# Spare products of the identity on TensorE, in the last attention batch and at the start of the experts

## The chip, the cores and the metric

The kernel runs on one NeuronCore of a Trainium2 chip. The metric is the time of one execution on the device in microseconds. The engines are TensorE (PE in the profile; PEld is its loading of weights), VectorE (DVE), ScalarE (ACT), GpSimd (POOL) and SyncE (SP), each with its own queue of instructions, tied to the others by semaphores. TensorE's clock is granted by the chip at one of two levels, 1.2 and 2.4 GHz; the profile gives the granted clock as a share of the full one.

## The reference

One decoder block over x of 4 x 512 tokens by 512 features, in float32:

```
x = x + attention(layernorm(x))     # 16 heads of 32, a band of 128 keys and 4 sinks, biases, output projection
x = x + experts(layernorm(x))       # silu(h @ c.T) * (h @ c.T) @ c, with c = ctx[expert of the token's id], 4 experts
x = x + bit_ffn(layernorm(x))       # 8-bit activations, ternary weights, hidden size 2048, rms norm
```

In the expert part the matrix c of 512 x 512 is the gate, the up and the down weight at once.

## The kernel before

The kernel has three phases that follow each other. The change touches the end of the first and the start of the second.

**Attention** (`attention_phase`). The four batches are worked one after another. Within a batch, four groups of four heads (g) by four tiles of 128 queries (qt) make 16 units. The round of a batch is g = 1 to 4; g = 4 is the first group of the next batch, so the last batch (b = 3) has rounds g = 1 to 3 only. PE's order is written out in `unit` (line 1026). Unit (g, qt) first makes the scores of the next unit into `s_ps` (`scores`, line 945: three products per head, float32 split in a high and a low part, then the band's mask), which waits until ACT has exponentiated the scores before them. Then it transposes the first two of its own four slots of probabilities (`transpose_slot`, line 967), does one product of a projection on the side (`side`, line 931: parts X, Q, K, V and O, into the bank `side_ps`), transposes slots three and four, and after every second unit multiplies the transposed probabilities by V (`attend_pair`, line 1009; the last products are those of the sinks). Slots one and three go through the first half of `pT_ps` and are copied out by ACT, slots two and four through the second half and are copied out by DVE; so slot three waits for ACT's copy of slot one, slot four for DVE's copy of slot two. In the last unit of a group the fourth slot is the widened reciprocal of the sums.

DVE's order per unit is in its own `unit` (line 749): the two maxima of the next unit's scores (line 725), the norm of the group before in units (g, 0), the copy of slot two, the side work, the copy of slot four; in units (2,1), (2,2), (2,3) and (3,0) of the last batch also an addition of the output bias to `xres` (line 797). ACT's is in line 570: the copy of slot one, four exponentials with their sums, the copy of slot three. POOL widens the reciprocals, splits the attention output in high and low (lines 412 to 424) and, in the last batch, splits the experts' matrices (lines 453 to 465), which are four large operations on 128 x 2048 elements on POOL and two on DVE.

In the last batch the side work ends with K3, the projection of the last keys, in unit (1,3); DVE ends its split with line 651 and counts `side_left` up. Units (2,0) to (3,1) have no side work. In unit (3,2) PE begins the output projection (`o_begun`, line 1020) into `side_ps` and free banks of `s_ps`; its last part, after the last split, is line 1085. Then the phase's block of programs ends: all engines meet, after SP and ACT have stored the last rows.

**Experts** (`expert_phase`). POOL gathers the tokens' rows by expert in 19 tiles of 128 (line 1317). For each tile DVE makes the statistics and normalizes (lines 1410 to 1424), PE transposes (`transpose_x`, line 1504), ACT and DVE make the high and low part (lines 1370 and 1428), PE multiplies by c (`expert_product`, line 1516: 12 matmuls of 128 x 512 into `z_ps`), ACT applies silu (line 1387), DVE multiplies (line 1464), PE transposes the result (line 1554), and 12 further matmuls make y (`y_of`, line 1526). PE's order is that of `tensor_program` (line 1503): the sums of the weights' absolute values (line 1534), then ten products of the identity with itself into `y_ps` whose result nobody reads (line 1536, the number is `KEPT_BUSY["experts"]` of line 37), the first transpose, and the loop over the tiles.

Of the kernel before, what the change touches and what calls it, by code (L numbers as in the profile page):

```python
# [10 lines left out]
P = 128  # L11
BATCH, SEQ, D = 4, 512, 512
# [3 lines left out]
HG = HEADS // GH  # L16
# [17 lines left out]
OWN_TILES = ROUTED_TILES - 2 * TT - FRONT_HOMES  # L34
X_LATE = 11
GATHERS_AHEAD = 6
KEPT_BUSY = {"experts": 10}
ROUTE_COUNTED, ROUTE_STEPS, ROUTE_DENSE = 10, 34, 42
LISTED = 2
BO_UNITS = [(2, 1), (2, 2), (2, 3), (3, 0)]  # L40
# [19 lines left out]
def attention_phase(nc, io, x1, x2, slot_tokens, dense_tokens, sh):  # L60
# [7 lines left out]
    with ExitStack() as ctx:  # L68
# [3 lines left out]
        def ps(name, shape, dt=F32):  # L72
            return ctx.enter_context(nc.psum_tensor(name, shape, dt))

        def sem(name):
            return ctx.enter_context(nc.semaphore(name))

        ident, rows, expert_of = sh["ident"], sh["rows"], sh["expert_of"]
# [73 lines left out]
        pT_ps = ps("pT_ps", [P, 2, GH * P])  # L152
        pv_ps = ps("pv_ps", [P, SEQ])
        side_ps = ps("side_ps", [P, SEQ])
# [9 lines left out]
        side_done, side_hi, side_left = sem("side_done"), sem("side_hi"), sem("side_left")  # L164
# [41 lines left out]
        def place_of(qt):  # L206
            return slice(QUERY_PLACE[qt] * P, QUERY_PLACE[qt] * P + P)
# [21 lines left out]
        def taken(b, name):  # L229
            return name not in LATE if b == 0 else name in LAST if b == BATCH - 1 else True  # L230
# [16 lines left out]
        def projected(b, g, qt):  # L247
            name = PROJECTED[g].split()[qt]
            return None if name == "-" or (g and not taken(b, name)) else name
# [32 lines left out]
        with nc.Block() as block:  # L282
# [608 lines left out]
            def _(pe):  # L891
                def product(out, steps, first, final):

                    terms = [(lt[i], r[j]) for lt, r in steps for i, j in ((0, 0), (0, 1), (1, 0))]
                    for n, (lt, r) in enumerate(terms):
                        last = nc.tensor.matmul(out, lt, r, start=(first and n == 0), stop=(final and n == len(terms) - 1))  # L896
                    return last
# [6 lines left out]
                def project(name, out, blocks_):  # L904

                    i = int(name[1])
                    rows, cols = slice(i * P, i * P + P), slice(i * P, i * P + P)
                    if name[0] == "O":
                        rows = place_of(i)
                    steps = []  # L910
                    for k in blocks_:
                        if name[0] in "QK":
                            n = name[0].lower()
                            steps.append(((w_hi[n][:, k, cols], w_lo[n][:, k, cols]), (xT_hi[:, k, :], xT_lo[:, k, :])))
                        elif name[0] == "V":
                            steps.append(((xT_hi[:, k, rows], xT_lo[:, k, rows]), (w_hi["v"][:, k, :], w_lo["v"][:, k, :])))
                        else:
                            steps.append(((aT_hi[:, k, rows], aT_lo[:, k, rows]), (w_hi["o"][:, k, :], w_lo["o"][:, k, :])))
                    return product(out, steps, blocks_[0] == 0, blocks_[-1] == DK - 1)
# [47 lines left out]
                def transpose_slot(b, g, qt, k):  # L967
                    slot = slots_of(qt)[k]
                    if copies_before(b, g, qt, k):
                        pe.wait_ge(slot_copied[k % 2], copies_before(b, g, qt, k))  # L970
                    if k == 0:
                        pe.wait_ge(exp_done, units_before(b, g, qt) * GH + GH)
                    if slot == "rinv":
                        pe.wait_ge(rinv_widened, b * HG + g + 1)
                        for t in range(TT):
                            last = nc.tensor.transpose(pT_ps[:, 1, place_of(t)], norm[:, t * P:t * P + P], ident[:])
                    elif slot == "sink":
                        pe.wait_ge(sinks_gathered, 2 * (b * HG + g) + qt - 1)
                        last = nc.tensor.transpose(pT_ps[0:GH * SINKS, 0, 0:P], sinks[:].rearrange("p h n -> p (h n)"), ident[:])
                    else:  # L980
                        a, z = columns(qt, slot)
                        for h in range(GH):
                            last = nc.tensor.transpose(pT_ps[:, k % 2, h * P:h * P + P], weights[qt][:, h, a:z], ident[:])  # L983
                    last.then_inc(slot_transposed, 1)
# [35 lines left out]
                def o_begun(t):  # L1020
# [2 lines left out]
                        pe.wait_ge(attn_split, BATCH * HG - 1)  # L1023
                    project(f"O{t}", o_banks[t], whole[:-1])

                def unit(b, g, qt, last):
                    nxt = (g, qt + 1) if qt + 1 < TT else (g + 1, 0)
                    if not (last and nxt == (HG, 0)):
                        scores(b, *nxt)
                    transpose_slot(b, g, qt, 0)  # L1030
                    transpose_slot(b, g, qt, 1)
                    name = projected(b, g, qt)
                    if name:
                        side(b, nth_in(b, g, name), name)
                    if last and g == HG - 1 and qt >= 2:
                        o_begun(qt - 2)
                    transpose_slot(b, g, qt, 2)
                    transpose_slot(b, g, qt, 3)
                    if last and (g, qt) == (HG - 1, TT - 1):
                        o_begun(2)  # L1040
                    if qt % 2:
                        attend_pair(b, g, qt - 1)
                    name = turned(b, g, qt)
                    if name:
                        side(b, nth(b, name), name)
# [37 lines left out]
                pe.wait_ge(attn_split, BATCH * HG)  # L1083
                for t in range(TT):
                    project(f"O{t}", o_banks[t], whole[-1:]).then_inc(o_projected, 1)


def landed(s):
# [136 lines left out]
def expert_phase(nc, ctx, scratch, io, x1, x2, sh, front):  # L1225
# [19 lines left out]
    ident, rows, expert_of = sh["ident"], sh["rows"], sh["expert_of"]  # L1245
# [18 lines left out]
    gate = big("gate", [P, D])  # L1264
# [5 lines left out]
    y_ps = front.y_ps  # L1270
# [20 lines left out]
    def inside(s):  # L1291
        return 0 <= s < ROUTED_TILES
# [210 lines left out]
    def tensor_program(pe):  # L1503
        def transpose_x(s):
            pe.wait_ge(xn_ready, s + 1)
            if inside(s - 1):
                pe.wait_ge(xT_lo_ready, s)
            for k in range(DK):
                last = nc.tensor.transpose(xT_ps[:, k, :], xn[:, s % 2, k * P:k * P + P], ident[:])  # L1509
            last.then_inc(xn_transposed, 1)  # L1510

        def weights_of(s):

            return nc.tensor.value_load(expert_of[0:1, one(s)], min_val=0, max_val=(EXPERTS - 1) * DK)

        def expert_product(out, hi, lo, first):

            n = 0
            for k in range(DK):
                at = bass.ds(first + k, 1)  # L1520
                for lt, r in ((hi, c_hi), (hi, c_lo), (lo, c_hi)):
                    last = nc.tensor.matmul(out, lt[:, k, :], r[:, at, :], start=(n == 0), stop=(n == 3 * DK - 1))  # L1522
                    n += 1
            return last

        def y_of(s):
            first = weights_of(s)

            pe.wait_ge(aT_lo_ready, s + 1)
            expert_product(y_ps[:], aT_hi, aT_lo, first).then_inc(y_ready, 1)  # L1530

        pe.wait_ge(consts, 3)
        pe.wait_ge(row_summed, 1)
        nc.tensor.matmul(sum_ps[:], e_ones[:], abs_row[:], start=True, stop=True).then_inc(all_summed, 1)
        for n in range(KEPT_BUSY["experts"]):
            nc.tensor.matmul(y_ps[:, 0:P], ident[:], ident[:], start=True, stop=True)
        transpose_x(0)

        for s in range(ROUTED_TILES):
            first = weights_of(s)  # L1540
            pe.wait_ge(xT_lo_ready, s + 1)
            if inside(s - 1):
                pe.wait_ge(a_ready, s)
            expert_product(z_ps[:], xT_hi[:, s % 2], xT_lo[:, s % 2], first).then_inc(z_ready, 1)
            if s == 0:
                transpose_x(1)
            if inside(s - 1):
                y_of(s - 1)
            if s == ROUTED_TILES - 1:
                pe.wait_ge(front.consts, 4)  # L1550
                front.transpose_x(pe, 0)
            pe.wait_ge(a_ready, s + 1)
            for k in range(DK):
                last = nc.tensor.transpose(aT_ps[:, k, :], act_sb[:, k * P:k * P + P], ident[:])  # L1554
            last.then_inc(a_transposed, 1)
            if inside(s + 2):
                transpose_x(s + 2)

        pe.wait_ge(w_ready, CHUNKS)
        front.first_gate(pe)  # L1560
        y_of(ROUTED_TILES - 1)
        front.transpose_x(pe, 1)
# [427 lines left out]
```

## Time and profile before

| what | value |
|---|---|
| median of 3 runs | 792.04 us (791.56 to 792.66) |
| span of the profiled execution, first to last instruction | 789.9 us; its own time outside the profiler isn't shown |
| TensorE busy | 735.5 us, 93% of the span, 5130 matmul records |
| VectorE, ScalarE, GpSimd busy | 597.9, 471.4, 333.0 us |
| mean granted clock of TensorE | 0.976 of 2.4 GHz |

The span is divided by the page into 40 slices of 19.7 us. The last attention batch's units (2,0) to (3,3) lie between 398 and 449 us, the last output projection ends at 454.6, the experts' phase begins at about 457.6 and lasts until about 600. A float32 product of the identity stands as two matmul records, a transpose as one.

### The profile page before, as it was taken

To read this page: it belongs to the slowest core of one execution; us is meant where nothing else is said; L and a number is where in the kernel's file an instruction comes from. 1 tells how busy PE (TensorE), PEld (TensorE's weight loads), DVE (VectorE), ACT (ScalarE), POOL (GpSimd) and SP (SyncE) were. 2 spreads that over 40 slices of the span, in tenths; PEclk is the share of its full clock that TensorE was granted. 3 is DMA by queue.
4 is the path that set the end of the run, shared out by engine and by line. 5 is a ranking of instruction groups with operands and counts; after the bars stand their busy time and mean duration, and the time that the engine had idled before them with its cause. 6 is when DMAs were issued, how large, how long until landed. Compare 5 with 4: busy or idle time off the path is not lost. (4 is left out here: it accounts for less than half of the span.)

```text
span 789.9 us, 14108 instructions
## 1 busy us (share of the span) xinstructions
PE 735.5 (93%) x5130; PEld 509.0 (64%) x5130; DVE 597.9 (76%) x1102; ACT 471.4 (60%) x1024; POOL 333.0 (42%) x330
## 2 busy tenths in 40 slices
PE   5988999999999999999987959999998999999984
PEld 4766777777777777777755747888874444444431
DVE  6886766886668866766677547887888999999982
ACT  5555766666667666766555214444455777667761
POOL 2011204213142134454373343445546667777662
PEclk9999999999999999999997979999999999999998
DMA  9200021304030331215330075455430233333231
GB/s 319 108 1 28 27 66 70 108 28 161 28 108 28 108 134 54 81 55 189 107 108 1 2 252 198 176 194 202 149 120 31 53 82 94 88 99 97 77 80 54
DMA packets 55218, 78.33 MB, mean 99 GB/s; under 512 B 36335, under 2 KB 38383, under 8 KB 53424
## 3 DMA queue, kind: packets, MB, share of 16 engines
q1 hardware_dynamic: 46336, 51.99, 20.2%
q0 software_dynamic: 8528, 24.93, 9.1%
q8 instruction: 43, 0.70, 0.4%
q10 hardware_dynamic: 288, 0.52, 0.2%
q14 instruction: 23, 0.19, 0.1%
HBM read 56.92 MB, written 17.59 MB: 94 GB/s over the span
## 5 line engine op out<-in xcount | busy, mean ns | idle before, releaser
L556 ACT ACTIVATE probs<-s_ps,neg_max 128x512 f32<-128x512 f32 (+2 forms) x256 | 152.3, 610 | 20.3 <-DVE neg_max L725 18.6
L725 DVE TENSOR_REDUCE neg_max<-s_ps 128x2 f32<-128x1024 f32 (+2 forms) x128 | 124.5, 1014 | 33.1 <-PE s_ps L963 32.6
L983 PE MATMUL pT_ps<-ident,probs 128*128 128x128 f32 x832 | 116.6, 282 | 9.3 <-DVE probs L746 8.3
L568 ACT ACTIVATE probs<-pT_ps 128x512 f32<-128x512 f32 x96 | 57.4, 598 | 98.6 <-PE pT_ps L983 97.8
L983 PEld LDWEIGHTS pT_ps<-ident,probs 128*128 128x128 f32 x832 | 95.0, 145 | 24.7 <-DVE probs L746 11.0
L746 DVE COPY probs<-pT_ps 128x512 f32<-128x512 f32 x112 | 76.8, 685 | 36.8 <-PE pT_ps L983 36.8
L1681 POOL TENSOR_TENSOR xg_own<-h,ln_w_sb 128x512 f32<-128x512 f32 x64 | 83.9, 1322 | 33.9 <-DVE h L1767 33.8
L896 PE MATMUL side_ps<-w_hi 128*128 128x512 f32 x172 | 71.1, 414 | 0.0
L420 POOL TENSOR_TENSOR aT_hi<-norm,one_col 128x512 fp32r<-128x512 f32 x15 | 15.6, 1040 | 125.4 <-DVE norm L737 87.1
L896 PE MATMUL side_ps<-w_hi,w_lo 128*128 128x512 f32 x172 | 67.5, 392 | 0.0
L896 PE MATMUL side_ps<-w_lo,w_hi 128*128 128x512 f32 x172 | 67.1, 390 | 0.0
L1875 PE MATMUL y_ps<-w_tern,hqT 128*128 128x512 bf16 x240 | 61.0, 380 | 2.6 <-DVE v_next L1809 2.6
L1005 PE MATMUL pv_ps<-probs,v_sb 128*32 128x256 f32 (+1 forms) x896 | 53.0, 373 | 0.4 <-ACT probs L568 0.4
L556 ACT ACTIVATION_READ_ACCUMULATOR probs<-s_ps,neg_max 128x1 f32 x256 | 52.8, 206 | 0.0
L1724 ACT ACTIVATE hq<-hq_big,minus_offset 128x1024 bf16<-128x1024 f16 x30 | 33.1, 1143 | 30.9 <-DVE hq_big L1804 30.9
L412 POOL TENSOR_TENSOR norm<-rinv,one_col 128x512 f32<-128x512 f32 x16 | 16.7, 1042 | 82.4 <-DVE rinv L732 82.4
L1875 PEld LDWEIGHTS y_ps<-w_tern,hqT 128*128 128x128 bf16 x240 | 22.9, 98 | 28.1 <-issue 3.0
L1643 PE MATMUL e_xT_ps<-w_tern,xqT_home 128*128 128x512 bf16 x128 | 33.0, 380 | 6.8 <-DVE h L1767 6.2
L1773 DVE TENSOR_REDUCE hw_max<-xg_own 128x1 f32<-128x1024 f32 x32 | 38.7, 1209 | 0.2
L1005 PEld LDWEIGHTS pv_ps<-probs,v_sb 128*32 128x32 f32 x896 | 25.5, 111 | 18.0 <-issue 6.0
L896 PEld LDWEIGHTS side_ps<-w_hi,w_lo 128*128 128x128 f32 x172 | 32.3, 188 | 7.3
L1387 ACT ACTIVATE gate<-e_z_ps 128x512 f32<-128x512 f32 x19 | 11.4, 598 | 42.0 <-PE e_z_ps L1522 42.0
(285 smaller groups left out, 1800.1 us busy)
## 6 DMA issues: line engine op xcount, KB each, us to landing
w_piece<-w_ffn SPq DMA_DIRECT2D x24, 512.0 KB, 3.5
w_stage<-w_ffn SPq DMA_DIRECT2D x12, 1024.0 KB, 4.8
xres<-x POOLq DMA_DIRECT2D x4, 1024.0 KB, 5.7
xn<-x SPq DMA_DIRECT2D x3, 1024.0 KB, 8.5
x<-xres POOLq DMA_DIRECT2D x3, 1024.0 KB, 4.8
xn<-c SPq DMA_DIRECT2D x2, 1024.0 KB, 6.1
v_next<-c SPq DMA_DIRECT2D x2, 1024.0 KB, 7.9
xn<-x SPq DMA_DIRECT2D x4, 256.0 KB, 3.5
```

The lines of the kernel that those rows point to most:

```text
L556: nc.scalar.activation(weights[qt][:, h, at:at + width(qt)], s_ps[:, h, 0:width(qt)], ACT.Exp, bias=neg_max[:, qt % 2, h:h + 1], accum_out ...
L568: nc.scalar.activation(out, turned_p, ACT.Identity).then_inc(slot_copied[0], 1)
L725: nc.vector.tensor_reduce(neg_max[:, qt % 2, 2 * s:2 * s + 2], s_ps[:, 2 * s:2 * s + 2, 0:width(qt)], AX.X, ALU.max, negate=True).then_inc ...
L746: nc.vector.tensor_copy(weights[qt][:, :, a:z], pT_ps[:, 1, :].rearrange("p (h n) -> p h n", h=GH))\
L896: last = nc.tensor.matmul(out, lt, r, start=(first and n == 0), stop=(final and n == len(terms) - 1))
L983: last = nc.tensor.transpose(pT_ps[:, k % 2, h * P:h * P + P], weights[qt][:, h, a:z], ident[:])
L1005: last = nc.tensor.matmul(pv_ps[HD * h:HD * h + HD, to], v_sb[:, slot, f:f + HD], p, start=first, stop=final, tile_position=(0, HD * h))
L1643: last = nc.tensor.matmul(out[:], xqT[:, t % 2, k, :], weights[:, k, cols], start=(k == 0), stop=(k == DK - 1))
L1681: nc.gpsimd.tensor_tensor(hw[:, t % 2, c, :], h[:, t % 2, c, :], ln_w[:, c * CHK:c * CHK + CHK], ALU.mult)\
L1724: nc.scalar.activation(hq[:, cols], hq_code[:, cols], ACT.Identity, bias=minus_offset[:]).then_inc(hq_packed, 1)
L1773: nc.vector.tensor_reduce(hw_max[:, i, n:n + 1], flat(hw, i)[:, n * HALF:n * HALF + HALF], AX.X, ALU.max, apply_absolute_value=True).then_ ...
L1875: last = nc.tensor.matmul(sums_of(t), hqT[:, t % 2, k, :], down_w[:, k, :], start=(k == 0), stop=(k == FK - 1))
```

## The change

The dictionary of numbers gets four new entries and another value for the experts. In the last attention batch, in units (2,0) to (3,1), PE makes four products of the identity with itself ahead of the next unit's scores and four behind the transposes of the first two slots, into `side_ps`; ahead of the first four it waits until K3 has been taken out of that bank. Ten more are made into `pT_ps` behind the last output projection. In front of the first transpose of the experts stand 24 instead of ten, behind it nine, and behind the second transpose seven, all into `y_ps`. No result of them is read.

```
-KEPT_BUSY = {"experts": 10}
+KEPT_BUSY = {"unit": 4, "end": 10, "experts": 24, "first split": 9, "first gate": 7}
...
+                def keep_busy(bank, where):
+                    for n in range(KEPT_BUSY[where]):
+                        nc.tensor.matmul(bank, ident[:], ident[:], start=True, stop=True)
+
                 def unit(b, g, qt, last):
                     nxt = (g, qt + 1) if qt + 1 < TT else (g + 1, 0)
+                    spare = last and (2 <= g < HG) and (g, qt) < (HG - 1, 2)
+                    if spare:
+                        pe.wait_ge(side_left, nth(BATCH - 1, "K3"))
+                        keep_busy(side_ps[:, 0:P], "unit")
                     if not (last and nxt == (HG, 0)):
                         scores(b, *nxt)
                     transpose_slot(b, g, qt, 0)
                     transpose_slot(b, g, qt, 1)
+                    if spare:
+                        keep_busy(side_ps[:, 0:P], "unit")
                     name = projected(b, g, qt)
...
                 for t in range(TT):
                     project(f"O{t}", o_banks[t], whole[-1:]).then_inc(o_projected, 1)
+                keep_busy(pT_ps[:, 0, 0:P], "end")
...
         nc.tensor.matmul(sum_ps[:], e_ones[:], abs_row[:], start=True, stop=True).then_inc(all_summed, 1)
-        for n in range(KEPT_BUSY["experts"]):
-            nc.tensor.matmul(y_ps[:, 0:P], ident[:], ident[:], start=True, stop=True)
+
+        def keep_busy(where):
+            for n in range(KEPT_BUSY[where]):
+                nc.tensor.matmul(y_ps[:, 0:P], ident[:], ident[:], start=True, stop=True)
+
+        keep_busy("experts")
         transpose_x(0)
+        keep_busy("first split")
 
         for s in range(ROUTED_TILES):
...
             if s == 0:
                 transpose_x(1)
+                keep_busy("first gate")
             if inside(s - 1):
                 y_of(s - 1)
```

## Rows read from the trace of the kernel before

**Rows 1.** The page: the span.

```profile
span 789.9 us, 14108 instructions
```

**Rows 2.** Stretches: us, busy us (records) of PE, PEld, DVE, ACT, POOL, clock, DMA share, GB/s.

```profile
403.80:407.20 3.40, 3.40 (x26) 2.63 (x25) 1.67 (x3) 0.64 (x3) 3.32 (x3) 0.53 0.02 5
...
417.50:424.30 6.80, 5.95 (x45) 3.46 (x41) 4.67 (x8) 3.39 (x10) 1.04 (x1) 0.52 0.01 2
...
431.10:434.50 3.40, 3.12 (x16) 2.49 (x15) 3.09 (x4) 2.30 (x8) 3.40 (x2) 0.53 0.00 0
...
458.40:465.20 6.80, 5.27 (x25) 5.27 (x26) 2.38 (x7) 0.69 (x1) 5.12 (x8) 0.51 0.48 133
...
472.10:475.50 3.40, 1.98 (x12) 1.29 (x11) 2.73 (x6) 2.18 (x4) 0.42 (x1) 0.97 1.02 419
```

**Rows 3.** Timeline, the spares before: start, length (us), engine, instruction, [idle before].

```profile
459.93 0.58 PE L1534 MATMUL up_ps<-abs_row,e_ones 128*128 128x3 f32 x2 [5.33 <-POOL e_ones L1335]
460.38 4.62 PE L1536 MATMUL y_ps<-ident 128*128 128x128 f32 x20
```

**Rows 4.** Timeline of PE: transposes of (2,2) and (2,3), attend products of (2,3) and (3,3).

```profile
412.53 1.04 PE L983 MATMUL pT_ps<-ident,probs 128*128 128x128 f32 x8
...
416.65 0.51 PE L955 MATMUL s_ps<-k_hi,q_hi 32*128 32x512 f32 x4
...
417.75 1.97 PE L983 MATMUL pT_ps<-ident,probs 128*128 128x128 f32 x8
...
421.99 2.29 PE L1005 MATMUL pv_ps<-probs,v_sb 128*32 128x256 f32 x24
...
447.39 1.29 PE L1005 MATMUL pv_ps<-probs,v_sb 128*32 128x256 f32 x24
```

**Rows 5.** Timeline, PE and DVE: unit (2,0) and the start of (2,1).

```profile
398.28 0.50 PE L955 MATMUL s_ps<-k_hi,q_hi 32*128 32x512 f32 x3
...
398.91 0.21 DVE L651 SCALAR_TENSOR_TENSOR k_lo<-side_ps,bk_sb,k_hi 128x4 fp32r<-128x4 f32 x1
...
399.90 1.23 DVE L725 TENSOR_REDUCE neg_max<-s_ps 128x2 f32<-128x1024 f32 x1 [0.78 <-PE s_ps L963]
...
403.51 1.07 PE L983 MATMUL pT_ps<-ident,probs 128*128 128x128 f32 x4 [1.75 <-DVE probs L746]
```

**Rows 6.** Timeline, PE, DVE, POOL: units (2,1), (2,2), (3,0), (3,1).

```profile
409.76 3.61 POOL L458 TENSOR_TENSOR w_hi<-xn,one_col 128x2048 fp32r<-128x2048 f32 x1
...
410.02 3.90 DVE L797 TENSOR_TENSOR xres<-xres,bo_sb 128x512 f32<-128x512 f32 x1
...
411.73 0.40 PE L955 MATMUL s_ps<-k_hi,q_hi 32*128 32x260 f32 x4
...
413.84 1.29 DVE L725 TENSOR_REDUCE neg_max<-s_ps 128x2 f32<-128x520 f32 x2
...
429.47 0.66 PE L983 MATMUL pT_ps<-ident,probs 128*128 128x128 f32 x4 [1.75 <-DVE probs L746]
...
431.11 2.86 PE L983 MATMUL pT_ps<-ident,probs 128*128 128x128 f32 x12
431.77 1.82 DVE L725 TENSOR_REDUCE neg_max<-s_ps 128x2 f32<-128x776 f32 x2
...
436.76 0.39 PE L955 MATMUL s_ps<-k_hi,q_hi 32*128 32x260 f32 x4
```

**Rows 7.** Timeline of PE: the first matmul of the first expert product.

```profile
467.38 0.49 PE L1522 MATMUL e_z_ps<-w_hi,e_xT_hi 128*128 x1 [1.86 <-DVE e_xT_lo L1428]
```

**Rows 8.** The chain in order of time: start us, us, what.

```profile
467.38 4.60 PE e_z_ps L1522 x12
...
473.44 0.65 PE e_aT_ps L1554 x4
...
475.12 4.59 PE e_z_ps L1522 x12
...
483.35 2.76 PE e_z_ps L1522 x12
```

## The prediction

> **What bounds the kernel now.** I read four views, in this order. First the page: a span of 789.9 us [rows 1]; the median of the runs shown, 792.04, is 2.1 us above it, and I put the sum on that median. Then the stretches around the falls [rows 2]: the clock stands at its lower level, 1.2 GHz, in 403.8 to 407.2, 417.5 to 424.3 and 431.1 to 434.5 (last attention batch), and in 458.4 to 465.2 (start of the experts). The first two expert products are slow as well, 4.60 and 4.59 us for 12 matmuls that later take 2.76 [rows 8]. Each fall follows idle time of PE, each return follows steady work. The four stretches are 20.5 us; half clock can have cost no more than half of that and the 3.7 us of the two products, and less where PE waits for others anyhow. Third, the timeline of the last batch: per unit PE makes the scores, VectorE (DVE) takes two maxima, ScalarE (ACT) four exponentials, and PE's next scores need those. Both PE's order and DVE's set the pace. Last, the chain: it runs over DVE to the first expert product [rows 7] and from there almost wholly over PE [rows 8], so what is lost or won there reaches the end whole.
>
> **The price of a spare product.** Ten products stand as 20 records in 4.62 us, the last record's own tail included: 0.43 us each at 1.2 GHz [rows 3]. No row has one at 2.4 GHz. Eight transposes of the same 128x128 shape take 1.97 us at the low clock and 1.04 at the high one [rows 4], so I take half: 0.21 us each, 0.85 for four. The bounds are 0.85 and 1.7 for four; I take the low one, as the spares follow other work of PE.
>
> **Part 1, four in front of the scores, units (2,0) to (3,1).** PE stood idle before none of these scores (no idle time is written beside them [rows 4 to 6]): its waits lie before the later transposes. So these four lie on the path.
> - Unit (2,0). The new wait is for K3's split, which DVE ends at 398.91 + 0.21 = 399.12; in the profile the scores began at 398.28, and DVE idled 0.78 us until it could start the maxima at 399.90 [rows 5]. Now the scores start at about 399.15 + 0.85 = 400.0: +1.75 us. Behind the waiting PE stand only these scores; DVE and ACT wait for them.
> - Unit (2,1). +0.85. What the clock gives back: from the last transposes to the scores two units on took 403.51 to 411.73, 8.22 us, against 429.47 to 436.76, 7.29, in the next round, where less of it was slow: -0.93. Near zero in sum.
> - Unit (2,2). Here DVE's addition to xres took 3.90 us next to POOL's 3.61 us copy of an expert's matrix, which had begun 0.26 earlier, and ended 0.55 after it; the maxima came only at 413.84, while the scores (from 411.73) were done about 1.1 us before [rows 6]. The four fit in that 1.1. POOL's work hangs on DVE's norm of unit (2,0), so it comes later by the same 1.75. Shift stays +1.75.
> - Unit (2,3). +0.85, as the scores start at 416.65 behind the transposes with nothing between [rows 4]. Back at full clock: about 0.15 in the scores, 0.5 in the four transposes of the reciprocals (half of 1.97 less 1.04), 1.0 in the attend products (24 took 2.29 here, 1.29 at full clock [rows 4]). Sum +1.75 + 0.85 - 1.65 = +0.95.
> - Unit (3,0). +0.85, and 0.1 because scores no longer overlap the products of the sinks: +1.9.
> - Unit (3,1). +0.85, of which DVE hides about 0.5: it took the maxima at 431.77 only, while PE had left the scores for the transposes at 431.11 [rows 6]. The slow transposes there (2.86 us for 12) lie beside DVE's maxima. Sum about +2.2.
> After it no spare is put in and the clock was full until the end of the stage: the stage ends **2.2 us later**. If the clock falls all the same, nothing comes back: 1.75 + 0.85 + 0 + 0.85 + 0.95 + 0.35 = +4.75, and up to about +8 with the fours behind the first at 1.7 each. If DVE's addition slips in ahead of POOL's copy (the 0.26 us above), about 0.5 less.
>
> **Part 2, four behind the first transposes of these units.** PE waits there for DVE anyhow, 1.75 us before the fourth slot's transposes in units (2,0) and (3,0) [rows 5, 6]; in (2,1) and (3,1) up to 0.2 us could show. Taken as zero; at 1.2 GHz 1.7 us would fill the whole cover.
>
> **Part 3, ten behind the output projection.** PE is idle for 5.33 us, from 454.6 until it is wanted at 459.93 [rows 3]. Ten at 0.21 take 2.1 us, or 4.3 at most. Zero, as the gather and the stores hide it. They leave 3.2 us of idle time, not 5.3; a slow product followed on 1.86 us of idle time as well [rows 7], so I don't count on their holding the clock.
>
> **Part 4, 24 instead of ten, nine behind the first transpose.** Times here are from the spares' start at 460.38. In the profile ten took about 4.3, and the first expert product began at +7.0, behind DVE's low part of the transposed row [rows 7]. Of the stretches at the lower level two lasted 3.4 us and two 6.8 [rows 2]. With 3.4 us of it the 24 take 8 x 0.43 + 16 x 0.21 = 6.8; with 4.86 (460.38 to 465.24, as here) 7.5; all low 10.3; all high 5.1. I take 6.8. Then four transposes (0.5), and nine spares (1.9, where the path over ACT's and DVE's copies took 1.86 [rows 7]): the product begins at +9.25, which is 2.25 us later. Given back: its 12 matmuls take 2.76 instead of 4.60 us [rows 8], -1.84.
>
> **Part 5, seven behind the second transpose.** 0.45 + 1.5 us, where the path over ACT and DVE to the transposed product takes 1.45 [rows 8]: +0.5. The second expert product then runs at full clock: 2.76 for 4.59, -1.83. Sum of parts 4 and 5: 2.25 - 1.84 + 0.5 - 1.83 = **-0.9 us**. From there on PE is busy and at full clock as before.
>
> **Sum.** +2.2 - 0.9 = +1.3, over 792.04: 793.3 us. About 0.2% (1.6 us) is what a measurement of this kernel can tell from no change; the forecast lies just inside it.
>
> A rule that speaks against the change: the row shows that in 431.1 to 434.5 PE did next to nothing but transposes, and that the clock was back at 434.5 [rows 2, 6]. The Trainium skill, "TensorE: Matmul & The Clock Gate", Part 4: PE-mode transpose, says that transposes don't count as busy time for the clock. By it four spares between long rows of transposes could be too little and the clock would fall in the units all the same; the trace disagrees in the place named. The time that this would give is the first rival's.
>
> **The rivals.**
> 1. *Slower: the clock falls in the units all the same*, since a spare group of 0.85 us leaves PE idle for the rest of each wait. Place: units (2,0) to (3,1). Price: +4.75 for the stage (above), -0.9 behind it: 795.9. Against it: with 0.85 of the 1.75 us waits filled, no unbroken idle time of the length seen before a slow stretch is left. For it: in 472.1 to 475.5 PE was busy for 1.98 of 3.4 us, in pieces [rows 2], and the product from 475.12 on was slow [rows 8]. It decides from two falls left in the units on.
> 2. *Slower, milder: the 24 run mostly at 1.2 GHz.* They end at +9 to +10.3 instead of +6.8: +2.2 to +3.5 over the forecast, 795.5 to 796.8. For it: the ten of the profile ran so from first to last [rows 3]. Against it: the clock was back 4.9 us after they began.
> 3. *Faster: the front four cost less than written*, because DVE is what PE waits for in more units than (2,2) and (3,1), for instance where DVE gets ahead of POOL, and because other executions lost more to the low clock than the profiled one. Stage +0.2, experts -2.6 (the 24 all at full clock, 5.1 us, so 1.7 less): 789.6. For it: up to 13 us stand to be won. Against it: the wait in unit (2,0), which nothing hides.
> 4. *The change doesn't do what it says:* the falls at the experts' start stay as they are, spares gain nothing there: +2.2 and +2.75: 797. Against it: steady spares brought the clock back at 465.2.
>
> **How the numbers follow.** Forecast and its neighbourhood (791 to 794.5) 0.55; rival 1 0.12; rival 2 0.10; rival 3 0.18; rival 4 0.05. Range: from 789.6 (rival 3's figure) to 796.2 (rivals 1 and 2); it leaves out rival 4 and the tails. Faster by over 0.2% (below 790.5): most of rival 3 and a little of the forecast's lower side, 0.18. Slower (above 793.6): rivals 1, 2, 4 and a third of the forecast, 0.40. Same: 0.42.
>
> **What the changed profile would show.** Right: no stretch at 1.2 GHz in units (2,0) to (3,1); 32 records of spares per pair of units at about 0.11 us apart; the maxima of unit (2,0) about 1.8 us later against the batch's start; PE's last output projection 2.2 us later; an idle stretch of some 3 us after the ten; the first expert product some 9.3 us after its spares' start; both first expert products in 2.76 us. Wrong: idle time of PE in front of the spares of other units than (2,0) (then they are hidden), the maxima at their old distance, falls between 398 and 435, or a first expert product more than 10 us behind the start of its spares.

## The result, and the profile after

The changed kernel took 795.16 us (median of 6 executions, 794.14 to 796.57), the kernel before on the same chips 791.57 (6, 786.52 to 792.66). The ratio is 1.0074, with a 95% interval of 1.0048 to 1.0099: 0.7% slower. The six times of the kernel before are far apart (three at 791.6 to 792.7, one at 786.5), so the two medians differ by 3.6 us only, while the ratio stands for 5.9. Repeated, it was 794.64 against 788.49 (6 and 26 executions), ratio 1.0070 (1.0042 to 1.0098), which is 5.5 us by the ratio and 6.2 by the medians. I had forecast +1.3 us; it is about +6.

Of the page after, the span and TensorE's granted clock in 40 slices:

```profile
span 794.8 us, 14443 instructions
...
PEclk9998999999999999999999999999999999999997
```

The spans differ by 4.9 us. The stretches of the changed kernel answer to [rows 2]; columns are us, busy us (records) of PE, PEld, DVE, ACT, POOL, clock, DMA share, GB/s:

```profile
398.00:403.80 5.80, 5.58 (x60) 3.65 (x60) 2.24 (x5) 2.54 (x9) 3.60 (x1) 1.00 0.35 142
403.80:435.00 31.20, 26.69 (x273) 21.25 (x272) 23.18 (x28) 17.29 (x50) 13.18 (x7) 1.00 0.11 36
435.00:459.00 24.00, 23.58 (x191) 17.34 (x190) 14.01 (x22) 7.55 (x23) 10.11 (x4) 1.00 0.02 6
459.00:464.40 5.40, 2.40 (x21) 2.20 (x19) 1.07 (x3) 1.28 (x1) 1.29 (x4) 1.00 0.47 173
464.40:467.80 3.40, 3.30 (x15) 3.31 (x16) 1.03 (x3) 0.00 (x0) 2.00 (x4) 0.50 0.59 159
467.80:484.00 16.20, 16.01 (x114) 14.54 (x113) 8.90 (x21) 3.51 (x7) 7.06 (x12) 1.00 0.90 329
```

The clock is at 2.4 GHz through all units and both first expert products. In this part of the kernel one fall of 3.4 us is left, at the start of the experts' spares. So the change does what it says, and the kernel is slower.

The timeline of the changed kernel (PE, DVE, POOL; start, length, engine, instruction, idle before) answers to [rows 5, 6]:

```profile
401.51 1.16 PE L1028 MATMUL side_ps<-ident 128*128 128x128 f32 x8 [0.22 <-DVE k_lo L651]
...
403.82 2.36 DVE L725 TENSOR_REDUCE neg_max<-s_ps 128x2 f32<-128x1024 f32 x2 [2.36 <-PE s_ps L963]
...
409.96 1.84 DVE L725 TENSOR_REDUCE neg_max<-s_ps 128x2 f32<-128x776 f32 x2 [1.15 <-PE s_ps L963]
413.75 4.10 DVE L797 TENSOR_TENSOR xres<-xres,bo_sb 128x512 f32<-128x512 f32 x1
...
413.69 3.61 POOL L458 TENSOR_TENSOR w_hi<-xn,one_col 128x2048 fp32r<-128x2048 f32 x1
...
417.78 1.29 DVE L725 TENSOR_REDUCE neg_max<-s_ps 128x2 f32<-128x520 f32 x2
```

DVE's idle time ahead of the first maxima grew from 0.78 to 2.36 us: that is the wait for K3 and the four spares. The addition to xres begins 0.06 us behind POOL's copy and waits for it. The chain of the changed kernel at the start of the experts, in order of time, answers to [rows 8]; the last line is not of the chain but of PE's timeline and answers to [rows 7]:

```profile
465.08 6.84 PE y_ps L1549 x48
471.93 0.44 PE e_xT_ps L1520 x4
472.36 2.01 PE y_ps L1549 x18
474.37 2.77 PE e_z_ps L1533 x12
477.14 0.44 PE e_xT_ps L1520 x4
477.57 1.56 PE y_ps L1549 x14
479.13 0.44 PE e_aT_ps L1571 x4
...
474.13 0.48 PE L1533 MATMUL e_z_ps<-w_hi,e_xT_hi 128*128 x1
```

Here the chain runs over the spares themselves; before, it ran over the gather and DVE.

The next table is worked out from the timelines: differences between the starts of DVE's first maxima of consecutive units (the unit's number is that of the scores they read), then from the start of the sum's matmul (the instruction ahead of the experts' spares) to the first expert product z0, from there to the second z1 and to the first y. The first column is from the maxima of the second batch's first unit to those of (2,1); the last is the sum of the columns. The starts of z0, z1 and y0 are those of the timeline. From (3,3) to the sum's matmul it was 22.3 us in all of them, which is left out.

| kernel, profiled execution | to (2,1) | (2,1) to (2,2) | to (2,3) | to (3,0) | to (3,1) | to (3,2) | to (3,3) | to z0 | to z1 | to y0 | sum |
|---|---|---|---|---|---|---|---|---|---|---|---|
| before | 266.19 | 6.32 | 7.62 | 4.08 | 7.94 | 5.91 | 5.88 | 7.44 | 7.74 | 4.43 | 323.55 |
| before, again | 266.18 | 5.25 | 5.93 | 4.15 | 6.53 | 5.91 | 7.59 | 7.39 | 7.52 | 2.86 | 319.31 |
| changed | 267.78 | 6.14 | 7.82 | 4.52 | 7.83 | 6.15 | 5.93 | 9.63 | 6.07 | 2.86 | 324.73 |
| behind the transposes only | 266.23 | 5.26 | 5.94 | 4.16 | 6.52 | 5.91 | 5.88 | 7.44 | 6.11 | 2.86 | 316.31 |

Against the first row the change costs 1.2 us, as forecast (+1.3). The other 3.7 us of the span lie where no spare stands: 2.2 in the first batch, where the changed execution had two falls of the clock (at 58.2 and 71.9) and the first one had one (65.7), and 1.5 at the end, where it had one more (775.0). But the first row is not what the kernel before usually does: its second profiled execution, the second row, is 4.2 us better in the same stretches. In the four jobs of the experiments the kernel before ran 119 times beside the others, with a median of 789.1; only 12 of these reached 791.5, the region of all three times I had.

### The profile page after: what moved, and what is told of

Read it like the earlier page. It is cut to its first block and busy times, and to the rows that moved or that the text cites. A ratio compares the mean times of both kernels' runs of the same rounds, so it can differ in the third digit from the quotient of the medians.

```text
span 794.8 us, 14443 instructions
## 1 busy us (share of the span) xinstructions
PE 746.8 (94%) x5289; PEld 522.5 (66%) x5306; DVE 598.9 (75%) x1102; ACT 471.7 (59%) x1024; POOL 333.1 (42%) x330
## 3 DMA queue, kind: packets, MB, share of 16 engines
q1 hardware_dynamic: 46336, 51.99, 20.5%
## 5 line engine op out<-in xcount | busy, mean ns | idle before, releaser
L983 PE MATMUL pT_ps<-ident,probs 128*128 128x128 f32 x832 | 112.6, 275 | 8.2 <-DVE probs L746 7.7
L983 PEld LDWEIGHTS pT_ps<-ident,probs 128*128 128x128 f32 x832 | 91.8, 141 | 22.4 <-DVE probs L746 10.3
L896 PEld LDWEIGHTS side_ps<-w_hi 128*128 128x128 f32 x172 | 32.4, 188 | 5.8 <-DVE k_lo L651 0.6
```

## The experiments

The experiments ran in four jobs, and the kernel before ran beside the others in each; ratios are against it. Medians of different jobs differ by some tenths of a microsecond for the same kernel: the kernel before had 788.87, 788.49, 789.45 and 788.93.

**The kernel before again, and the change in two halves.**

> The kernel before, unchanged, as a control. Theory A (the clock's falls move from run to run): its times spread over several us again, between about 786 and 793 as so far, and the profile shows its falls of the granted clock in other places than the first one did, with the last batch's VectorE and GpSimd operations shifted against each other. Theory B (the changed kernel pays somewhere that no spare stands): the times stay near 792 and the falls stand where they stood.

Measured: 789.38 us (785.4 to 794.02, 12 executions); ratio 1.0012 (0.9987 to 1.0038), the kernel compared with itself. Its profile has the clock low at 427.9 to 434.7 and nowhere else in the units. Its addition, by the timeline of DVE and POOL:

```profile
409.74 1.44 DVE L797 TENSOR_TENSOR xres<-xres,bo_sb 128x512 f32<-128x512 f32 x1
...
410.58 4.05 POOL L458 TENSOR_TENSOR w_hi<-xn,one_col 128x2048 fp32r<-128x2048 f32 x1
```

It came 0.84 us ahead of the copy, and this time POOL waited. Its 1.44 us, where such an addition takes 0.68 elsewhere, are a wait as well: POOL's operation ahead of the copy ran until 410.63. So theory A holds: the falls move from execution to execution, and with them this order.

Only the spares in the units:

```
-KEPT_BUSY = {"unit": 4, "end": 10, "experts": 24, "first split": 9, "first gate": 7}
+KEPT_BUSY = {"unit": 4, "end": 0, "experts": 10, "first split": 0, "first gate": 0}
```

> Only the four and four spares in units (2,0) to (3,1). Theory A (my sum, each part priced against the falls of one execution): from the end of K3's split to PE's last output projection 2.1 us more than the 55.5 us of the first profile, the experts' start as slow as before; over the median of before by about 3, since the median execution lost less to the clock in the units than the profiled one. Theory B (the cost lies in the experts' part): within 1 us of before.

Measured: 792.84 us (12) against 788.87, ratio 1.0057 (1.0034 to 1.0080). From the end of K3's split to the last output projection it took 57.7 us for 55.5, as theory A said; against the median of before it is 4.0 us slower, where A said about 3. The profile shows the addition at 4.10 us. So most of the loss lies here.

Only the spares around the experts (`spare = False`, the numbers of the changed kernel else):

> Only the ten behind the output projection, the 24, nine and seven; none in the units. Theory A: 1.1 us less than before from the spares' start to the second tile's matmuls if the first two expert products are at 1.2 GHz in before, up to 2.5 us more if they are at full clock there anyhow; median within 1.5 us of before. Theory B: slower by 3 or more, as the first expert product waits for the spares.

Measured: 788.49 (12), ratio 0.9987 (0.9963 to 1.0011). No loss and no gain that can be told. In its profile the clock didn't fall at the experts' start at all; PE's timeline there:

```profile
461.73 5.61 PE L1549 MATMUL y_ps<-ident 128*128 128x128 f32 x48
```

The 24 took 5.6 us, last record's tail included, and z0 came 8.05 us after the sum's matmul. The units of this kernel are those of before, and this execution (792.01, the slowest of its twelve) looks like the first profile there: falls at 405.3, 418.9 and 432.6, and the addition 0.02 us behind the copy and 4.14 us long. In both, the fall near 404 had made the step from (2,1) to (2,2) longer than the 5.25 us of full clock, by 1.07 and 0.84 us. Less the 0.84 us by which the addition is ahead at full clock, this makes it 0.2 and 0.0 us late, where the rows have 0.26 and 0.02. So in the kernel before, the clock's fall itself can turn the order.

**The spares behind the transposes alone.** The four in front of the scores are left out, and so are all the experts' new ones:

```
-                    if spare:
-                        pe.wait_ge(side_left, nth(BATCH - 1, "K3"))
-                        keep_busy(side_ps[:, 0:P], "unit")
                     if not (last and nxt == (HG, 0)):
...
                     if spare:
+                        pe.wait_ge(side_left, nth(BATCH - 1, "K3"))
                         keep_busy(side_ps[:, 0:P], "unit")
```

> Only the four spares behind the first two slots' transposes in units (2,0) to (3,1), with the wait for K3's split moved there (free, as the split is done by then). Theory A: PE waits there anyhow, so they cost nothing; the clock may be held in part of the falls; 0 to -2 us against before. Theory B (every spare delays the chain): +2 to +5 us.

Measured: 785.27 (784.47 to 786.28, 12), ratio 0.9954 (0.9936 to 0.9972): faster than both kernels, and its 12 times spread over 1.8 us where the 35 of before spread over 9.7. The stretch of its units:

```profile
398.00:435.00 37.00, 31.82 (x361) 24.00 (x350) 26.90 (x38) 21.72 (x64) 24.31 (x10) 1.00 0.10 30
```

The clock is at full speed without one product in front of any scores. The last row of the table is what the units take then. Against it the products in front cost 1.6 us up to unit (2,1) and 4.7 from there to (3,3), 6.3 us in the profiles. Step by step the 4.7 are 0.9, 1.9, 0.4, 1.3, 0.2 and 0.1: the second is the step with the late addition, and the fourth is 0.4 more than four products, which no run here explains. By the medians of this job (792.84 and 785.27) the products in front cost 7.6 us, so their price is known to about a microsecond.

**The changed kernel again, and the addition moved out of the way.**

> The changed kernel, unchanged, for a ratio over many executions. Theory C (the fours in front of the scores make VectorE's addition to xres in unit (2,1) come just behind the start of GpSimd's copy and so wait for all of it, 4.1 us instead of 1.4, in every execution; before pays that in some executions only): 0.4 to 0.7% slower than before, with a narrow spread of its own but for falls of the clock in the first batch and at the end; the addition takes about 4.1 us in the profile. Theory A (only the sum of the parts as forecast, +1.3): 0.1 to 0.2% slower.

Measured: 794.64 (793.78 to 795.59, 6), ratio 1.0070 (1.0042 to 1.0098). The addition took 4.10 us again, in the same place.

```
-BO_UNITS = [(2, 1), (2, 2), (2, 3), (3, 0)]
+BO_UNITS = [(2, 2), (2, 3), (3, 0), (3, 2)]
```

> The changed kernel with VectorE's four additions of the bias in units (2,2), (2,3), (3,0) and (3,2) instead of (2,1), (2,2), (2,3) and (3,0), so none stands where GpSimd copies the experts' matrices in unit (2,1). Theory C: from the maxima of unit (2,0) to those of unit (2,2) 11 to 12 us instead of 13.96; 2 to 3 us faster than the changed kernel. Theory A: no change beyond 0.7 us (the addition itself).

Measured: 793.76 (9), ratio 1.0067 (1.0046 to 1.0089). A miss for theory C in its size: from (2,1) to (2,3) it took 13.17 us for 13.96, not 11 to 12; from (2,2) to (2,3) 7.03 for 7.82. Once the addition is gone PE is what the maxima wait for: its four spares of unit (2,2), which had lain in the addition's shadow, come out.

> The same move in the kernel before. Theory C: the executions in which the addition came late disappear, the median falls by 1 to 2 us and the highest of the times by 2 or more. Theory A: same as before, with the same spread of some 9 us, as the clock alone makes it.

Measured: 788.19 (784.98 to 789.5, 12), ratio 0.9984 (0.9966 to 1.0002). The highest time fell as theory C said (789.5, where 8 of the 26 times of the kernel before in the same job lie above it, up to 792.19). The median fell by 0.3, not by the 1 to 2 that C said. This fits a late addition that makes the tail of before, and in part of its executions only; twelve times are few to show it.

One product fewer in front of unit (2,1):

```
-                        keep_busy(side_ps[:, 0:P], "unit")
+                        keep_busy(side_ps[:, 0:P], 3 if (g, qt) == (2, 1) else "unit")
```

> The changed kernel with three products instead of four in front of the scores of unit (2,1), and nothing else. The addition began 0.06 us behind GpSimd's copy in the changed kernel; one product less is 0.25 us. Theory C: the addition now comes about 0.2 us ahead and takes 1.4 us; 1.5 to 3 us faster than the changed kernel for one product less, at least in most executions. Theory A: 0.25 us faster.

Measured: 793.63 (12), ratio 1.0059 (1.0041 to 1.0076). The addition slipped ahead (0.78 us long). (2,1) to (2,3) took 12.95 us for 13.96: one product of 0.22 us brought 1.0, again cut short by the four of unit (2,2).

**The same threshold where nothing else covers it.** To the spares behind the transposes four or three products are added in front of unit (2,1) alone:

```
+                    if last and (g, qt) == (2, 1):
+                        pe.wait_ge(side_left, nth(BATCH - 1, "K3"))
+                        for n in range(4):
+                            nc.tensor.matmul(side_ps[:, 0:P], ident[:], ident[:], start=True, stop=True)
```

> The spares behind the transposes, and four in front of the scores of unit (2,1) alone. VectorE's addition began 0.83 us ahead of the start of GpSimd's copy without them, and four products are 0.86 us. Theory D: the addition falls behind the start of the copy and waits for it, 4.1 us for 1.4; from the maxima of unit (2,1) to those of (2,2) 8 us instead of 5.9, in all 2.7 to 3 us slower than 785.3. Rival (the products cost only their own time): 0.9 slower.

> As the kernel with four in front of unit (2,1), with three. Theory D: the addition stays 0.2 us ahead of the copy and takes 0.7 to 1 us; 0.7 us slower than 785.3 at most, so one product, 0.22 us of PE's time, is worth 2 us or more here. Rival: 0.22 us between three and four.

Measured: 789.54 with four (12; ratio 0.9998, 0.9981 to 1.0015), 787.10 with three (12; 0.9972, 0.9954 to 0.9991). The timelines of DVE and POOL, with four:

```profile
406.24 1.84 DVE L725 TENSOR_REDUCE neg_max<-s_ps 128x2 f32<-128x776 f32 x2 [1.15 <-PE s_ps L963]
410.03 4.09 DVE L797 TENSOR_TENSOR xres<-xres,bo_sb 128x512 f32<-128x512 f32 x1
414.04 1.29 DVE L725 TENSOR_REDUCE neg_max<-s_ps 128x2 f32<-128x520 f32 x2
...
409.97 3.60 POOL L458 TENSOR_TENSOR w_hi<-xn,one_col 128x2048 fp32r<-128x2048 f32 x1
```

and with three:

```profile
406.95 1.84 DVE L725 TENSOR_REDUCE neg_max<-s_ps 128x2 f32<-128x776 f32 x2 [0.93 <-PE s_ps L963]
410.74 0.76 DVE L797 TENSOR_TENSOR xres<-xres,bo_sb 128x512 f32<-128x512 f32 x1
412.88 1.31 DVE L725 TENSOR_REDUCE neg_max<-s_ps 128x2 f32<-128x520 f32 x2 [1.39 <-PE s_ps L963]
...
410.91 4.05 POOL L458 TENSOR_TENSOR w_hi<-xn,one_col 128x2048 fp32r<-128x2048 f32 x1
```

With four the addition begins 0.06 us behind the copy and the maxima follow 7.80 us after the last ones; with three it begins 0.17 ahead and they follow after 5.93. Together with the products themselves, four cost 2.8 us from (2,1) to (2,3) and three 0.7. The fourth, 0.22 us of PE, costs 2.1 us in the profiles and 2.4 by the medians. Theory D holds: this pair of kernels differs by one product and by the order it sets. Both medians are about 1.2 us higher than expected; the kernel before was 0.6 higher in this job too, and the rest isn't accounted for.

**The wait in unit (2,0), and all but the front.**

> The spares behind the transposes, and four in front of the scores of unit (2,0) alone, behind the wait for K3's split. Theory D: the maxima of unit (2,0) come 1.6 us later, nothing else moves, median 786.9. Rival (the wait is hidden behind VectorE's split, which uses the same engine): within 0.9 of 785.3.

Measured: 788.45 (12), ratio 0.9988 (0.9969 to 1.0007). The path up to (2,1) took 267.79 us for 266.23, +1.56, and the columns from there to (3,3) are those of the table's last row: the mechanism and its price as said. The median is 1.5 above the 786.9 expected; in the profile the step from z0 to z1 took 7.71 us for 6.11, as the clock fell there, which is this much, but whether it does so in most executions wasn't seen.

> The changed kernel without any of the 24 products in front of scores (the fours behind the transposes, the ten, 24, nine and seven all stay). Theory D (the loss lies in the products in front of the scores, 6.3 us with the wait for K3's split and with VectorE's late addition; the 24 cost 2 us or more beyond what they give back once the clock is held anyway): median about 787.5, 6 to 7 us faster than the changed kernel and 2 to 2.5 slower than the spares behind the transposes alone (785.3). Rival (the experts' spares pay for themselves): at or below 785.3.

Measured: 788.15 (12), ratio 0.9986 (0.9965 to 1.0007). Near theory D's 787.5 (it is 3.0 us above the fours behind alone, for the 2 to 2.5 of the theory), and 6.5 us below the changed kernel's 794.64 of the other job (6.6 by the two ratios). In its profile the clock didn't fall at the experts' start, and z0 came after 8.05 us.

**Which of the experts' spares cost.** Each group is added by itself to the spares behind the transposes (only the numbers of `KEPT_BUSY` differ).

> The spares behind the transposes alone, again, beside variants on the same chip. Theory D (they hold the clock in the units at no cost): 3 to 4 us faster than before again, spread under 3 us. Rival (the first result was a lucky phase of the clock): within 2 us of before, spread of 4 us or more.

> The same and the ten products behind the output projection. Theory D: hidden, 0; if they shorten the fall of the clock so that the first ten of the experts' spares and the first two expert products run at full clock, up to 1.6 us faster in the executions where those are slow otherwise. Rival: they hold up the end of the stage, slower by 1 or more.

> The spares behind the transposes, and 24 instead of ten at the experts' start, without the ten, nine and seven. Theory D: the first expert product begins 7.6 to 9.5 us after the spares' start, where it is 7.5 with ten, since the 24 outlast the gather and the normalization when they start at 1.2 GHz; 0.5 to 2 us slower than the spares behind the transposes alone. Rival: the held clock gives it back, no slower.

> The spares behind the transposes, ten at the experts' start as before, and nine and seven behind the first two transposes. Theory D: nine and seven lie almost wholly in PE's waits (0.1 and up to 0.5 us show) and keep the first two expert products at full clock: 0 to 1 us faster than the spares behind the transposes alone in executions where those products were slow, else 0.4 slower. Rival: they delay both products, 1 us or more slower.

| kernel | median us | ratio to before | 95% interval |
|---|---|---|---|
| behind the transposes | 785.16 (6) | 0.9955 | 0.9938 to 0.9971 |
| and ten at the end of attention | 786.37 (12) | 0.9969 | 0.9958 to 0.9981 |
| and 24 for the ten of the experts | 788.17 (12) | 0.9996 | 0.9985 to 1.0008 |
| and nine and seven | 785.86 (6) | 0.9958 | 0.9943 to 0.9973 |

The gain repeats. The ten are not shown to help or to cost: their profile is that of the base (z0 after 7.48 us in both). The nine and seven are free within what can be told. The 24 cost 3.0 us (2.8 by the means). The timeline of PE with the ten of before, then with the 24, both behind the fours of the units:

```profile
458.30 4.62 PE L1547 MATMUL y_ps<-ident 128*128 128x128 f32 x20
462.70 1.06 PE L1518 MATMUL e_xT_ps<-ident,e_xn 128*128 128x128 f32 x4
```

```profile
457.05 8.14 PE L1547 MATMUL y_ps<-ident 128*128 128x128 f32 x48
465.03 0.60 PE L1518 MATMUL e_xT_ps<-ident,e_xn 128*128 128x128 f32 x4
```

The 24 hold the first transpose until 8.0 us after their start, the ten until 4.4. z0 comes 10.59 us after the sum's matmul for 7.48, and z1 and y0 follow in the same 6.1 and 2.86 us in both. In these two there was nothing left for the 24 to give back. It isn't so in every execution: of the six profiles with the fours behind, ten at the experts' start and neither nine nor seven, two (with four in front of unit (2,0), and with three in front of (2,1)) had the first expert product slow, and z0 to y0 took 10.5 us there.

## Why the prediction was wrong

The forecast was "same", +1.3 us (793.3), and it came out at 795.2, some 6 us above what the kernel before usually takes. The range held the median of 795.16. That it would be no change, and the size, did not hold.

- **What was right.** Against the profiled execution every part came out near its number. Up to unit (2,1) +1.6 (forecast 1.75). From there to (3,3) the changed kernel took 38.39 us for 37.75, +0.6, and with the first part +2.2, as written. A spare product costs 0.22 us at full clock. Its z0 came 9.19 us after the spares' start (464.94 to 474.13; forecast 9.25). From z0 to y0 8.93 us for 12.17. No falls in the units, 3.1 us of idle time behind the ten.
- **The step that failed: "I put the sum on that median", with the give-back priced by the falls of one execution ("-0.93" in unit (2,1), "-1.65" in (2,3), "-1.84" and "-1.83" at the experts).** The falls lie elsewhere in every execution; one in a unit cost between nothing and 1.7 us (7.59 for 5.88), as some lie where others set the pace. I gave the change the savings of an execution that had lost most: 3 stretches low in the units and both expert products slow. Of the 4.1 us by which the first profile's six columns from (2,1) to (3,3) exceed the last row's (37.75 less 33.67), the second profile had lost 1.7. Over many executions, all that the kernel before loses to the low clock in the units, with what hangs on it (the late addition, a slow first expert product), is the 3.8 us between it and the fours behind the transposes (788.93 and 785.16). My sum gave back 2.6 us in the units and 3.7 at the experts, 6.3. My rival 3 had "other executions lost more to the low clock"; they lost less.
- **The second step: "Unit (2,2) ... The four fit in that 1.1", and "about 0.5 less" for the addition slipping ahead.** I took the late addition of the first profile, 0.26 us behind POOL's copy, as how the kernel runs. It is one of two cases, and it needed the fall near 404: of three profiles with these units it was late in two, and both were slow executions for their kernel. By the times (median 789.1, 12 of 119 at 791.5 or more) it is the less usual case, but no run counts it. At full clock the addition comes 0.84 us ahead of the copy, and the four in front of unit (2,1), 0.86 us, use up just that. So in (2,1) and (2,2) the products in front cost 2.8 us (13.96 for 11.18) against a kernel whose clock is full there, not the nothing that I had for them together. The 0.26 us stood in my rows, and I saw it only as a chance for the changed kernel, not as a doubt about the row of before.
- **The third, a size: "I take 6.8" for the 24.** The time hangs on how long the clock is low there, and six profiles with the ten behind the output projection had all three cases: 5.6 us at full clock (two of them, z0 8.05 us after the sum's matmul), about 7 with 3.4 us of low clock (6.98 and 7.23 with the tail, z0 after 9.6 to 9.7), about 8.2 with 6.8 us of it (8.16 and 8.22, z0 after 10.8 to 10.9). The 24 without the ten took 8.14. The bound of 10.3 was not reached. Against ten spares (z0 after 7.4 to 7.6) the cost is thus 0.6 to 3.4 us, 3.0 by the medians of the one pair, and most of what it was to buy was already there: with the units at full clock, z0 to y0 takes 8.97 us with ten spares too, in four of six profiles.
- **Two sums.** The parts of "Slower" (rivals 1, 2 and 4 and a third of the forecast) add up to 0.45, not 0.40, and what "stand[s] to be won" (half of 20.5, and 3.7) is 14 us, not 13. Neither changes the forecast.
- **The rivals.** 1 and 4 are excluded by the clock's rows. 2 has half a truth, with 8.0 for its 9. None had the mechanism of the addition on the slower side.

The sum by the runs: from the fours behind the transposes (785.2) the products in front add 6.3 by the profiles and the 24 add 3.1: 794.6, measured 794.64. The kernel before is 3.8 above the same base. The difference, 5.6, is the size of the loss measured (5.5 to 6.2). That it meets so closely is in part luck, as the terms are not so well known: 7.6 for the first by the medians, 0.6 to 3.4 for the second.

By the rule that the prediction weighed (the Trainium skill, "TensorE: Matmul & The Clock Gate", Part 4: PE-mode transpose), transposes don't count as busy time for the clock, and four spares among them could have been too little. The clock did not fall in the units: four spares of 0.86 us per unit, between 16 transposes of 0.11 us, the scores and the attend products, came with the clock's upper level in the units in 13 of the 14 profiles that have them. The other is the one with four in front of unit (2,1) alone, where PE waits longer for the late addition; it fell at 417.1. Whether the transposes counted, or the rest was enough, no run here separates.

## What to carry to other kernels

Filler work belongs behind what the engine's partner is already working on, not ahead of what it waits for: the same product was free in one place of the unit and cost its full time, or ten times that, in the other. Before a trace is used as the base of a sum, ask which of its rows another execution would show otherwise: a clock that falls in other places, or two operations of different engines that start within less than a microsecond of each other (here 0.26 in one execution, 0.84 in another); then price the change against both orders. And when two measures buy the same thing (here the clock at the experts' start), the second has mostly its cost.

## What was not expected of the hardware

- DVE's addition of two tensors in SBUF and POOL's large copy exclude each other whole, in the order of arrival: 4.09 us for DVE when it began 0.06 us late, 0.76 us for DVE and 4.05 instead of 3.60 for POOL when it began 0.17 us early. The Trainium skill, "SBUF — State Buffer", section "SBUF: two separate sides", says that DVE (with two SBUF inputs) and a GpSimd operation lock their shared port pair for a whole instruction and the other fully blocks. The trace agrees: the late addition took 3.41 us more than its usual 0.68, and 3.54 of the copy were left when it began. DVE's maxima, which read PSUM, ran at their usual 1.84 us beside POOL's 4.54 us operation.
- The 35 executions of the kernel before in one job spread over 9.7 us (784.06 to 793.74). With the fours behind the transposes alone it was 1.8 us (12 executions) and 2.8 (6), and 1.4 to 4.8 in the seven kernels that add something to them. Outside the units, a fall near the end cost 1.3 to 1.5 us in each of the six profiles that had one (195.2 to 195.4 us from the experts' last product to the end, for 193.9 to 194.0). The first batch took 2.0 us more in the changed kernel's first profile with two falls (108.7 us between the first maxima of its first two batches); another profile with two falls there took 106.9, where the rest took 106.3 to 107.2, so that cost hangs on where they lie. And the first maxima come between 26.8 and 28.9 us in the 18 profiles, 2 us of spread ahead of the first fall that any of them shows.
